# A decoder of twelve sublayers on one core: idle dense products in TensorE's waits, and narrow products spread among dense ones

## The reference

```
x = x + _L0_attn_ref(_layernorm(x, axis=-1), ...)     # gated delta rule, six heads, causal convolutions
x = x + _L0_xattn_ref(_layernorm(x, axis=-1), ctx, ctx)  # grouped cross-attention, 32 query and 8 key heads
x = x + _L0_ffn_ref(...)     # eight experts, the two best of each token, with biases
x = x + _L1_attn_ref(...)    # a linear recurrence over the sequence
x = x + _L1_xattn_ref(...)   # latent cross-attention, 16 heads
x = x + _L1_ffn_ref(...)     # eight gated experts with low-rank parts
x = x + _L2_attn_ref(...)    # causal attention, 16 heads
x = x + _L2_xattn_ref(...)   # latent cross-attention, 16 heads
x = x + _L2_ffn_ref(...)     # 32 masked experts, one per token
x = x + _L3_attn_ref(...)    # latent attention, 16 heads
x = x + _L3_xattn_ref(...)   # as in layer 0
x = x + _L3_ffn_ref(...)     # low-rank experts, one per token
```

## Time and profile before

| | |
|---|---|
| median of 3 runs | 1398.31 us (1396.41 to 1400.75) |
| the profiled execution's own time | 1398.4 us |
| its span, from first to last instruction | 1396.7 us |
| mean granted clock of TensorE | 0.955 |
| busy: PE, PEld | 91%, 69% |
| busy: DVE, ACT, POOL | 56%, 42%, 27% |
| moved by DMA | 67.8 MB, 49 GB/s on average |

### The profile page before, as it was taken

How to read it: one execution, slowest core, us unless ns; L and a number is a source line. 1 busy time by engine, 2 the same in 40 slices (tenths; PEclk the granted TensorE clock), 3 DMA queues, 4 the chain that set the end, 5 groups by cost and what they waited for, 6 DMA issues and landing times. The chain is left out here.

```text
span 1396.7 us, 29908 instructions
## 1 busy us (share of the span) xinstructions
PE 1266.5 (91%) x12533; PEld 963.0 (69%) x12533; DVE 778.3 (56%) x1473; ACT 593.1 (42%) x1078; POOL 371.0 (27%) x306
## 2 busy tenths in 40 slices
PE   6989998979989998999988888999988968999988
PEld 3469995558977567788857758788775435676555
DVE  4664565553344572633347655888735675863542
ACT  3632334473555474533332441223433363663451
POOL 0154303015641000555520004444202134523000
PEclk9979999988999999999998988999999999999989
DMA  4000003027006000100056080000016312200000
GB/s 115 1 2 4 4 4 122 1 80 151 1 1 204 1 2 1 35 0 1 1 137 180 1 254 1 2 1 2 2 66 207 124 44 50 55 21 31 2 1 31
DMA packets 78421, 67.81 MB, mean 49 GB/s; under 512 B 22344, under 2 KB 74256, under 8 KB 78160
## 3 DMA queue, kind: packets, MB, share of 16 engines
q1 hardware_dynamic: 75472, 63.10, 15.9%
q0 software_dynamic: 768, 2.10, 0.5%
q10 hardware_dynamic: 2048, 0.70, 0.2%
HBM read 53.30 MB, written 8.39 MB: 44 GB/s over the span
## 5 line engine op out<-in xcount | busy, mean ns | idle before, releaser
L1893 PE MATMUL ps<-rounded 128*128 128x512 f32 x384 | 91.3, 393 | 2.0 <-POOL rounded L1924 1.0
L1296 POOL TENSOR_TENSOR fixed<-fixed,cross 128x768 f32<-128x768 f32 x32 | 58.9, 1841 | 109.5 <-DVE cross L1245 109.5
L1210 PE MATMUL ps<-rounded 128*128 128x256 f32 x576 | 79.8, 294 | 6.8 <-DVE rounded L1264 4.1
L1893 PEld LDWEIGHTS ps<-rounded 128*128 128x128 f32 x384 | 70.9, 188 | 20.4 <-POOL rounded L1924 5.4
L1210 PEld LDWEIGHTS ps<-rounded 128*128 128x128 f32 x576 | 73.5, 197 | 10.9 <-issue 4.7
L1924 POOL TENSOR_TENSOR rounded<-weights,rounded 128x256 fp32r<-128x256 f32 x32 | 23.7, 761 | 185.0 <-ACT rounded L1942 185.0
L211 PE MATMUL ps<-fixed 128*128 128x128 f32 x160 | 35.3, 342 | 39.6 <-ACT fixed L199 30.4
L1275 ACT COPY cross<-ps 128x256 f32<-128x256 f32 x32 | 11.9, 373 | 116.0 <-PE ps L1219 116.0
L211 PEld LDWEIGHTS ps<-fixed 128*128 128x128 f32 x160 | 20.4, 166 | 53.5 <-issue 23.0
L1815 DVE SCALAR_TENSOR_TENSOR fixed<-ps,work,fixed 128x256 f32<-128x256 f32 x64 | 28.0, 479 | 51.5 <-PE ps L1725 51.5
L2031 DVE TENSOR_TENSOR work<-work,ps 128x512 f32<-128x512 f32 x32 | 22.0, 688 | 62.1 <-ACT work L1959 60.0
(11 more groups left out here) (492 smaller groups left out, 3117.3 us busy)
## 6 DMA issues: line engine op xcount, KB each, us to landing
weights<-in_L_ffn_masksT SPq DMA_DIRECT2D x32, 256.0 KB, 6.5
weights<-in_L_ffn_fc_w SPq DMA_DIRECT2D x16, 256.0 KB
weights<-in_L_xattn_Wq SPq DMA_DIRECT2D x2, 2048.0 KB, 9.8
weights<-in_L_xattn_WoT SPq DMA_DIRECT2D x2, 2048.0 KB, 10.2
work<-work SPq DMA_DIRECT2D x64, 64.0 KB, 2.0
sorted_in<-work SPq DMA_DIRECT2D x1, 3072.0 KB, 14.7
work<-sorted_in SPq DMA_DIRECT2D x12, 256.0 KB, 2.8
sorted_out<-work SPq DMA_DIRECT2D x12, 256.0 KB, 2.2
```

The costliest lines, as they stand in the source:

```text
L1210: last = nc.tensor.matmul(seen[:, a, :], m[:, u % 2, c, a, :], of[:, c, part * D:(part + 1) * D], start=c == 0 and n == 0, stop=c == KC - ...
L1296: nc.gpsimd.tensor_tensor(ro[:, v % 2, :, :], ro[:, v % 2, :, :], sn, ALU.add).then_inc(s["roped"], 1)
L1893: last = nc.tensor.matmul(ps[:, 2 * (n % 2) + i, :], a[:, q % 2, i, c, :], b[:, c, half * BANK:(half + 1) * BANK], start=c == 0 and part = ...
```

## The change

18 new calls of `hold` (or larger ones) stand in PE's program: ahead of the transposes of norms and behind the last one (in `stage_gqa`, which runs twice, `attend`, `stage_L0_ffn`, `stage_L1_ffn`, `stage_L2_attn`), at the beginning of `attend_L2`, in `stage_L3_attn` and `stage_L2_attn`, and in three blocks of `stage_L0_attn`. The 16 narrow products of the first stage go in groups of four behind the halves of projections 1 and 2. In `stage_L0_ffn` the transposes of `comb` move ahead of the last six of expert 1's first products, and the bias products of a bank go one bank ahead of expert 0's second products. In `scores(0)` of `stage_L2_attn` a wait for the first two `keys` stands ahead of the idle products. Nothing changes on another engine, and no result changes.

```
--- before.py
+++ after.py
@@ -409,7 +409,9 @@
                 if 1 <= t <= NT:
                     weigh(t - 1, 1)
             for i in range(NT // 2):
+                hold(k, 6, (2, 0, 9, 0)[i])
                 norm_turn(k, s, pe, i, (0, 1))
+            hold(k, 6, 3)
 
         @block.gpsimd
         def _(pool):
@@ -674,7 +676,9 @@
                 if j > 1 and turned:
                     norm_turn(k, s, pe, j // 2 - 1, (6, 7))
         if turned:
+            hold(k, 2, 9)
             norm_turn(k, s, pe, NT // 2 - 1, (6, 7))
+            hold(k, 2, 3)
         else:
             hold(k, 6, 10)
 
@@ -1200,6 +1204,8 @@
         def project(pe, v):
             u, part = divmod(v, 4)
             pe.wait_ge(s["w_rest"], u + 1)
+            if v < 2:
+                hold(k, 7, 12 - 6 * v)
             if u == 0:
                 pe.wait_ge(s["h_rest"], part + 1)
             for a in range(3):
@@ -1415,6 +1421,8 @@
                 for i in range(4):
                     last = nc.tensor.transpose(ps[:, 4 * g + 2, i * P:(i + 1) * P], km[:, 4 * g + i, :], k.ident)
                 last.then_inc(s["t_km"], 1)
+                if g == 0:
+                    hold(k, 3, 13)
             hold(k, 7, 10)
             pe.wait_ge(s["c_lat"], 2)
             for n in range(8):
@@ -1678,6 +1686,13 @@
 
         @block.tensor
         def _(pe):
+            def bias_products(i):
+                for jj in range(2):
+                    j = 2 * i + jj
+                    last = nc.tensor.matmul(ps[:, 4 + i, jj * D:(jj + 1) * D], combT[:, j * P:(j + 1) * P], w.b2,
+                                            start=True, stop=True)
+                last.then_inc(s["bias"], 1)
+
             pe.wait_ge(w.sem, w.loaded)
             route_logits(k, pe, w.gate, E, s["logits"])
             for e in range(E + 1):
@@ -1697,22 +1712,19 @@
                                                             b[:, c, half * BANK:(half + 1) * BANK],
                                                             start=c == 0 and part == 0, stop=c == KC - 1 and part == 2)
                             last.then_inc(s["h1"], 1)
+                            if n == 6:
+                                pe.wait_ge(s["comb"], 1)
+                                for j in range(NT):
+                                    last = nc.tensor.transpose(ps[0:E, 5 + j // 4, (j % 4) * P:(j % 4 + 1) * P], comb[:, j, :], k.ident)
+                                last.then_inc(s["combT"], 1)
                 if e == 1:
-
-                    pe.wait_ge(s["comb"], 1)
-                    for j in range(NT):
-                        last = nc.tensor.transpose(ps[0:E, 5 + j // 4, (j % 4) * P:(j % 4 + 1) * P], comb[:, j, :], k.ident)
-                    last.then_inc(s["combT"], 1)
                     pe.wait_ge(s["cT"], 1)
-                    for i in range(4):
-                        for jj in range(2):
-                            j = 2 * i + jj
-                            last = nc.tensor.matmul(ps[:, 4 + i, jj * D:(jj + 1) * D], combT[:, j * P:(j + 1) * P], w.b2,
-                                                    start=True, stop=True)
-                        last.then_inc(s["bias"], 1)
+                    bias_products(0)
                 if e >= 1:
                     pe.wait_ge(s["d_rest"], e)
                     for i in range(4):
+                        if e == 1 and i < 3:
+                            bias_products(i + 1)
                         pe.wait_ge(s["a_rest"], 4 * e - 1 + i // 2)
                         if e >= 2:
                             pe.wait_ge(s["acc"], 8 * (e - 2) + 2 * i + 2)
@@ -1727,7 +1739,9 @@
                                                             stop=c == KC - 1 and part == 2)
                         last.then_inc(s["y"], 1)
             for i in range(NT // 2):
+                hold(k, 2, (0, 4, 4, 2)[i])
                 norm_turn(k, s, pe, i, (0, 1))
+            hold(k, 2, 3)
 
         @block.gpsimd
         def _(pool):
@@ -2448,8 +2464,13 @@
                 c, i = divmod(u, 4)
                 at = 6 * (u % 2)
                 if u == 0:
+                    pe.wait_ge(s["keys"], 2)
+                    hold(k, 4, 5)
                     pe.wait_ge(s["vals"], 4)
                     pe.wait_ge(s["keys"], 4)
+                elif u < 4:
+                    hold(k, 5, (0, 0, 6, 3)[u])
+                    pe.wait_ge(s["centred"], u - 1)
                 elif u >= 2:
                     pe.wait_ge(s["centred"], u - 1)
                 rows = slice(32 * i, 32 * i + 32)
@@ -2508,7 +2529,9 @@
                 if j % 2:
                     last.then_inc(s["out"], 1)
             for i in range(NT // 2):
+                hold(k, 6, (6, 3, 3, 2)[i])
                 norm_turn(k, s, pe, i, (4, 5))
+            hold(k, 6, 3)
 
         @block.gpsimd
         def _(pool):
@@ -2682,13 +2705,15 @@
                     for c in range(KC):
                         last = nc.tensor.matmul(ps[0:widths[n], 2 * (n % 3) + half, :], w.qkv[:, c, offs[n]:offs[n] + widths[n]],
                                                 k.hT[:, c, half * BANK:(half + 1) * BANK], start=c == 0, stop=c == KC - 1)
-                last.then_inc(s["proj"], 1)
-                if n == 2:
-                    for j in range(NT):
-                        for c in range(KC):
-                            last = nc.tensor.matmul(ps[:, 6, 12 * j:12 * j + 12], k.hT[:, c, j * P:(j + 1) * P], w.ba[:, c, :],
-                                                    start=c == 0, stop=c == KC - 1)
-                    last.then_inc(s["ba"], 1)
+                    if half:
+                        last.then_inc(s["proj"], 1)
+                    if n in (1, 2):
+                        for j in range(4 * n - 4 + 2 * half, 4 * n - 2 + 2 * half):
+                            for c in range(KC):
+                                narrow = nc.tensor.matmul(ps[:, 6, 12 * j:12 * j + 12], k.hT[:, c, j * P:(j + 1) * P], w.ba[:, c, :],
+                                                          start=c == 0, stop=c == KC - 1)
+                        if j == NT - 1:
+                            narrow.then_inc(s["ba"], 1)
                 for j in gated_with[n]:
                     if j == 0:
                         pe.wait_ge(s["bac"], 2)
@@ -2800,6 +2825,8 @@
                 for c in range(3):
                     last = nc.tensor.transpose(ps[:, j, c * P:(c + 1) * P], vf[:, c, j * P:(j + 1) * P], k.ident)
                 last.then_inc(s["vT"], 1)
+            pe.wait_ge(s["vc"], 1)
+            hold(k, 4, 14)
 
         @block.scalar
         def _(act):
@@ -2985,8 +3012,10 @@
             for h in range(2):
                 decays(h)
                 keys(h)
+                hold(k, 5, 3)
             for h in range(2):
                 queries(h)
+                hold(k, 5, 3)
             for h in range(2):
                 turn(h)
             for pair in range(3):
@@ -3324,7 +3353,7 @@
             turn(pe, 3)
             product(pe, 2)
             product(pe, 3)
-            hold(k, 0, 10)
+            hold(k, 0, 22)
```

65 lines of the change are left out of this document (47 added, 18 removed).

## The result

The changed kernel took 1376.56 us, median of four runs (1374.5 to 1379.9), beside 1397.36 for the kernel before, timed with it on the same chip: ratio 0.985, 95% interval 0.982 to 0.988, a gain of 21 us. A second set on another occasion gave 1374.84 and 0.985 (0.982 to 0.989). The forecast was 1371 us, with 1362 to 1384 as its range; the measured time lies inside it, at the upper edge of the 1365 to 1377 that the forecast took for its own.

What follows compares the result with a forecast made beforehand. TensorE, busy 91% of the span, was taken to bound the kernel, its clock at the lower level for 126 us. Ten terms summed to 30.8 us; 27 were taken, from 1398 to 1371 us, range 1362 to 1384.

Steps and rivals of the forecast that it cites:

- term 2: Before and in the recurrence: 14 idle products ahead, four groups of three inside, against low clock; saves 2.5 us (0.5 to 3.5).
- term 3: End of the first layer: 22 idle products instead of 10 before the grouped attention; saves 1.3 us (0 to 1.6).
- term 4: Norms of the two grouped attentions: nine idle products in a wait, router faster; saves 3.1 us and 2.3 us.
- term 6: Norms ending layer 0's and 1's experts and layer 2's attention: idle products in waits; saves 2.5 + 2.2 + 2.5 us.
- term 7: Ends of the two cross attentions: nine idle products in a wait; saves 2.2 us in layer 1, 0.6 in layer 2.
- Term 9: Beginning of layer 2's cross attention: idle products behind the wait delay the first projection; a loss, -0.8 us.
- Term 5: Bias products of layer 0's experts: spread, transposes earlier, full clock; saves 5.7 us (2.5 if the clock falls all the same).
- Term 1: First stage: narrow products in four bursts behind dense work, so the clock stays high; saves 2.5 us (1.6 to 2.7).
- Term 8: Layer 2's attention: faster turns and first weighting with idle products between units; saves 2.6 us (1 to 3).
- The caution: Whole kernel: 27 taken of the 30.8 us sum, as three or four of fourteen places would probably see the low level.
- The weighed rule: In the norms: the Trainium skill's statement that transposes do not count as TensorE activity like products; would give 1383 us.
- norms fall all the same: Rival: the clock still falls in the norms, so terms 4, 6 and 7 (15.4 us) go; 1383 us, chance 0.13.

Runs made afterwards that it cites:

- Experiment 4: Changed kernel without all idle products in the norms at the ends of stages: 1390.5 us, ratio 0.996 to the kernel before.
- Experiment 6: Changed kernel without the four groups of three idle products in the recurrence's steps: 1376.4 us, ratio 0.987 to the kernel before.
- Experiment 3: Changed kernel with idle products of layer 2's cross-attention ahead of the wait for weights, 14 for 12 in the first group: 1371.1 us, ratio 0.983.
- experiment 5: Changed kernel with each idle product in the norms replaced by two idle f32 transposes of 128x128: 1376.1 us, ratio 0.987.
- experiment 8: The changed kernel again, no edit: 1374.8 us.
- experiment 11: Changed kernel with the norms' idle products at 8 stationary columns in place of 128: 1372.7 us, ratio 0.984.
- experiment 1: Changed kernel with the bias products and comb transposes of the L0 experts back in the order of the kernel before: 1376.2 us, ratio 0.984.
- experiment 7: Changed kernel with finer-spread bias products, idle products between, and layer 2 cross-attention's idle products ahead of the weights' wait: 1368.6 us, ratio 0.982.
- experiment 10: Changed kernel with the norms' idle products contracting over 8 rows in place of 128: 1398.5 us, ratio 1.002.
- experiment 12: Kernel of experiment 7 with more idle products in layer 2's attention and around the routing wait of the L2 experts: 1373.6 us, ratio 0.984.

## Why the prediction was right, and where not

The direction, the mechanism and the range are right; the gain was 21 us of a sum of 30.8, and of the 27 that the forecast took. No error cancelled another of note: by the table three stages (L0's experts, layer 2's attention and its cross-attention) miss 9 of the 10.4 us that lack. The low level went from 126 to 38 us, and these 88 us less gave 21, where they would give 44 if all of it had been dense work on the path.

**What held.** Terms 2 (recurrence), 3 with the norm's part of 4 (grouped attention), 6 behind the L0 experts (L1's beginning), 7 in the L1 experts, 10 and the last stage came within 0.7 us of their size in the mean of two executions (table). Experiment 4 shows terms 4, 6 and 7 together: 14 us for 15.4. Experiment 6 shows, in one execution, that in the recurrence the small groups are needed, not only the 14 ahead of it: without them 2.1 of the 2.8 us are lost.

**Term 9** was right in its reason, and the loss too small. Its -0.8 was a net of what the clock gives and what the misplaced products take. The first projection starts 3.9 and 4.3 us after the first of the twelve idle products in the two executions, inside the 2.6 to 5.1 foreseen, and from that projection on the stage is 2.5 us shorter in the mean. With a wait for DVE that is 0.2 longer in the mean, this makes -1.8. The fold ahead of it gained 1.7, where term 6 had 2.2. Experiment 3 shows what taking the idle products out of the wait's way is worth: 3.4 to 4.8 us. The whole stage, for which terms 6, 7 and 9 made 1.7 us, gained nothing (-0.2).

**Term 5** is the largest that was mis-sized, and its failure is not the one that the first profile suggests. That profile alone (115.3 us, 13.7 at the low level) would say that the spreading gained nothing, since 2.1 us of the stage are no more than the router's; the second (109.2, none) that the stage gained 8.2 of its 8.5. Of six executions in which the block is as in the changed kernel and the clock was kept through the norm ahead of it (experiments 3, 5, 6, 8, 11 and the first) four had no low stretch in it (109.2 to 109.3 us) and two had one (110.7 and 115.3), mean 110.5. The kernel before had 117.4 and 114.6, mean 116.0. The stage's gain is so about 5.5 us where 8.5 were forecast. The step that failed is the one that set against each other the low stretch of one execution and none at all: "16 records ... 2.5 less", "2.1 less". The old order alone, with the clock kept by the norm and the router before it, took 111.2 (experiment 1). Experiment 4 is the other half: with the new order but bare norms the stage took 118.3 us with 22.7 at the low level, no less than before the change. So most of the 5.5 comes from what stands ahead, and the order of the bias products has about 1 us of it, which one execution of the old order can't settle. Its 48 dense records took 7.38 us, for 5.8 at the full clock; less this 1.6 the old order is at 109.6, an estimate, for 109.2 with the new one. The wait of 1.30 us that the new order saves (term 5 had 1.2 for it) is there mostly taken back by the block itself, which takes 10.3 us for 11.0 - 1.6 = 9.4 in the old order.

**Term 1** took 2.5 us from a fall of the clock that the kernel before doesn't have in its second execution (43.2 us, below both executions of the changed kernel). In all twelve executions with the spread products the first stage took 43.0 to 44.5 us without a low stretch, 43.9 in the mean; for the kernel before there are only its two, one with the fall and one without. What the spread products gain in the mean is open: 1.2 by two executions each, in no experiment alone.

**Term 8 with the norm's part of 6** gave 2.3 of 4.8. Term 6's part came: the stage's first 32 records took 13.97 us, for 15.88 and 16.05 before. So of term 8's own 2.6 us less than 0.5 was left. Layer 2's attention had 6.8 to 20.5 us at the low level in eight of the nine executions with the changed kernel's idle products in its units and a clock kept through the norms (all but experiment 7, with 3.4). Its scores contract over 32 rows, and dense idle products stood only between them. The forecast counted these stretches as fallen for want of work; the windows of experiments 8 and 10 show that PE can be busy and the clock fall. That it is the 32 rows that let it fall here is not shown: no experiment took them alone.

**The caution** of 3.8 us, for "three or four of the fourteen places", was of the right kind and too small: a low stretch comes back in layer 2's attention and in the L2 experts nearly always, in L0's experts and at L1's beginning at times.

**The weighed rule** (transposes don't count) would have led to 1383 us; experiment 5 shows it not to hold for f32 transposes. The rival "norms fall all the same" got 0.13 partly on its account.

## What to carry to other kernels

Fill a wait of TensorE ahead of the wait, not behind it, and with products that contract over all 128 rows; over 8 rows the same number of instructions took 26 us more than over 128 rows with 8 columns (numbers of rows between were not tried). Fill no more than the wait holds, and not where the next thing to come is a transfer: in experiment 12 the clock then fell behind it, in work that counts. Take the cost of a low stretch from several executions of each kernel, since its place and length in one are not a property of the kernel.

## What was not expected of the hardware

- One and the same kernel ran one block at 0.50 for 13.7 us in one execution and at 1.00 in another; the first stage of the kernel before likewise (6.8 us and none). The changed kernel's total varied by 5.4 and 5.0 us between the runs of its two sets.
- Idle products of 0.21 to 0.22 us kept the clock through the norms with a stationary 128x128 (1374.8 us in the second set) and 128x8 (1372.7), and pairs of f32 transposes did too (1376.1); a stationary 8x128 of the same length did not (1398.5; none at all: 1390.5).
- The kernel with the highest mean clock (0.995) was 5 us slower than one with 0.992.
